# The second stage of a linear-attention and mixture-of-experts block: sixteen groups written out, or six written out and ten in a loop

## The reference

```python
h = layernorm(x) * (1 + ca) + sa                     # x: 2 x 4096 x 512; ca, sa, ga, ... from silu(c) @ wmod
q, k = relu(h @ Wq.T), relu(h @ Wk.T); v = h @ Wv.T  # 16 heads of 32
out = (v' k) q, divided per head by sum(k) . q + 1e-15   # linear attention, no softmax
x1 = x + ga * (out @ w_proj.T + b_proj)
h2 = layernorm(x1) * (1 + cb) + sb
# router: rms norm, logits (8 experts), top 2, softmax weights
# experts: gelu(h2 @ gate) * (h2 @ up) @ down, weighted, summed over the two experts
return x1 + gb * moe(h2)
```

## Time and profile before

| | us |
|---|---|
| median of 3 runs | 2297.94 |
| lowest, highest | 2295.66, 2310.27 |
| the profiled execution | 2295.66 |
| its span, first to last instruction | 2293.9 |
| outside the span | 1.76 |

### The profile page before, as it was taken

How to read it: one execution, slowest core, us unless ns; L and a number is a source line. 1 busy time by engine, 2 the same in 40 slices (tenths; PEclk the granted TensorE clock), 3 DMA queues, 4 the chain that set the end, 5 groups by cost and what they waited for, 6 DMA issues and landing times.

```text
span 2293.9 us, 42231 instructions
## 1 busy us (share of the span) xinstructions
PE 2143.8 (93%) x9280; PEld 1632.9 (71%) x9281; DVE 1437.1 (63%) x3325; ACT 774.7 (34%) x1395; POOL 893.9 (39%) x684
## 2 busy tenths in 40 slices
PE   7999999999988999984899999999989989999997
PEld 5688878888655555552678887887778768778886
DVE  6555555555389999995356565665556556566664
ACT  4243434444334444442132222332223223223332
POOL 4475746656437777775011111111111111111111
PEclk9999999999999999997999999999999999999998
DMA  7576454565625665557755557557675785665554
GB/s 243 205 239 204 163 194 162 210 205 180 216 74 186 218 223 209 186 179 285 219 131 126 125 127 221 131 130 188 156 221 128 190 249 134 180 170 126 131 118 78
DMA packets 292793, 404.88 MB, mean 177 GB/s; under 512 B 50126, under 2 KB 188366, under 8 KB 284878
## 3 DMA queue, kind: packets, MB, share of 16 engines
q1 hardware_dynamic: 164720, 257.57, 35.0%
q0 software_dynamic: 30640, 74.29, 15.3%
q10 hardware_dynamic: 97200, 70.82, 9.6%
HBM read 210.57 MB, written 191.98 MB: 175 GB/s over the span
## 4 chain that ended last, share of the span: by engine, by line
PE 41%; DMA 6%; issue 2%; DVE 1%; ACTq 1%; SPq 1%; ACT 0%; DVEq 0%; POOL 0%
PE bank L1793 41%; DMA arow<-act_rows 3%; DMA act_rows<-hact 3%; ACTq L1044 1%; DVE hact L1682 0%; DMA wbuf<-expert_split 0%; SPq L552 0%; DVE gbr L1718 0%; DVE x_t_lo L1676 0%; DVE act_t_lo L1693 0%; DVEq L1700 0%; ACT gact L1033 0%; DMA expert_rows<-rows,dest 0%; DMA meta<-expert_rows 0%; SPq L550 0%
## 5 line engine op out<-in xcount | busy, mean ns | idle before, releaser
L1793 PE MATMUL bank<-wbuf,x_t_hi 128*128 x2160 | 682.2, 398 | 45.0 <-DVE x_t_lo L1676 41.3
L787 POOL DMA_INDIRECT out_rows<-orow,cur_tok x135 | 209.0, 1548 | 990.0 <-DVE orow L1721 891.0
L1793 PEld LDWEIGHTS bank<-wbuf,x_t_hi 128*128 128x128 f32 x2160 | 410.5, 190 | 139.6 <-issue 49.4
L1793 PE MATMUL bank<-wbuf,x_t_lo 128*128 x1080 | 426.0, 394 | 0.0
L1793 PE MATMUL bank<-wbuf,act_t_hi 128*128 x1080 | 346.7, 403 | 33.3 <-DVE act_t_lo L1693 33.1
L1682 DVE TENSOR_TENSOR hact<-bank,gact 128x512 f32<-128x512 f32 x135 | 93.3, 691 | 335.2 <-PE bank L1793 303.7
L1793 PEld LDWEIGHTS bank<-wbuf,act_t_hi 128*128 128x128 f32 x1080 | 208.1, 193 | 83.4 <-issue 37.8
L1793 PEld LDWEIGHTS bank<-wbuf,x_t_lo 128*128 128x128 f32 x1080 | 205.1, 190 | 47.3
L1793 PE MATMUL bank<-wbuf,act_t_lo 128*128 x540 | 215.9, 400 | 0.0
L1033 ACT ACTIVATE gact<-bank 128x512 f32<-128x512 f32 x135 | 80.7, 598 | 324.1 <-PE bank L1793 264.2
L750 POOL DMA_INDIRECT expert_rows<-rows,dest x128 | 133.8, 1046 | 105.3 <-DVE dest L1458 70.7
(11 more groups left out here) (224 smaller groups left out, 4102.2 us busy)
## 6 DMA issues: line engine op xcount, KB each, us to landing
wbuf<-expert_split SPq DMA_DIRECT2D x24, 1536.0 KB, 8.8
xrow<-expert_rows SPq DMA_DIRECT2D x540, 64.0 KB, 2.8
act_rows<-hact ACTq DMA_DIRECT2D x135, 256.0 KB
arow<-act_rows ACTq DMA_DIRECT2D x540, 64.0 KB
expert_split<-split_hi SPq DMA_DIRECT2D x32, 768.0 KB, 3.5
expert_split<-split_lo SPq DMA_DIRECT2D x32, 768.0 KB, 5.8
xg<-in_x SPq DMA_DIRECT2D x16, 1024.0 KB, 5.6
q_rows<-qf SPq DMA_DIRECT2D x16, 1024.0 KB, 6.5
```

The lines of the kernel that those rows point to most:

```text
L787: pool.indirect_dma_start(out=out, out_offset=bass.IndirectOffsetOnAxis(cur_tok[at][:, 0:1], 0), in_=orow[at % 2][:, :], in_offset=None, c ...
L1793: last = mm(dst, stationary(a, f), moving(b, f), start=(k == 0), stop=(k == parts * n - 1))
```

## The change

`run_groups2` now writes out groups 0 to 2 and 13 to 15, and runs groups 3 to 12 as five turns of a loop with two groups in each. In the loop g is a register, so:

- the values of the waits are worked out by register operations in front of the instructions that wait;
- the batch is `(g >> 3) & 1`, and what is chosen by it (`gab`, `modbc`, `kvp`) is addressed by a register;
- `denominators` no longer reads `ksums` of the batch. VectorE copies the batch's key sums into a new tile `ksum_now` (128 x 64) once for each group (`ksum_of`), and TensorE waits for that copy (`ksum_ready`) in place of the wait on `prep_step`. In a group, `ksum_of(g + 2)` stands between `rec_lo(g + 1)` and `residual(g, 0)`, and waits until the denominators of group g + 1 are done, since there is one tile. For groups 0 and 1 it stands ahead of the first group. There are 16 copies.

No arithmetic on the data changes.

```diff
@@ run_groups2 @@
-        for g in range(NG):
+        for g in range(3):
+            group2(g, g % 2)
+        with eng.Fori(1, (NG - 4) // 2) as j:
+            group2(2 * j + 1, 1)
+            group2(2 * j + 2, 0)
+        for g in range(NG - 3, NG):
             if before_last and g == NG - 1:
                 before_last()
             group2(g, g % 2)
@@
     def batch_of(g):
-        return g // GPB
+        return g // GPB if isinstance(g, int) else (g >> 3) & 1
@@ add_bias (POOL) @@
-                pool.tensor_tensor(xb[par][:, t, :], xb[par][:, t, :], gab[:, batch_of(g), :], ALU.add).then_inc(s_xb, 1)
+                b = batch_of(g)
+                row = gab[:, b, :] if isinstance(b, int) else gab[:, bass.ds(b, 1), :].rearrange("p a n -> p (a n)")
+                pool.tensor_tensor(xb[par][:, t, :], xb[par][:, t, :], row, ALU.add).then_inc(s_xb, 1)
@@ VectorE @@
+        def ksum_of(g):
+
+            at_least(dve, s_den, g)
+            if isinstance(g, int) and g == 2:
+                dve.wait_ge(s_prep, 3)
+            b = batch_of(g)
+            dve.tensor_copy(ksum_now[:, :, :], ksums[:, b, :, :] if isinstance(b, int) else
+                            ksums[:, bass.ds(b, 1), :, :].rearrange("p a f h -> p (a f) h")).then_inc(s_ksum, 1)
@@ mod_row_of (VectorE) @@
-            return modbc[:, batch_of(g), k, :]
+            b = batch_of(g)
+            return modbc[:, b, k, :] if isinstance(b, int) else modbc[:, bass.ds(b, 1), k, :].rearrange("p a n -> p (a n)")
@@ group2 (VectorE) @@
             if not last:
                 rec_lo(g + 1)
+            if has(g, 2):
+                ksum_of(g + 2)
             residual(g, 0, par)
@@ ahead of the groups (VectorE) @@
+        ksum_of(0)
+
         tt(rw[:, :, :], rw[:, :, :], rscale[:, :].unsqueeze(2).to_broadcast([P, FC, E]), ALU.mult).then_inc(s_prep, 1)
         for a in range(HG):
             kvp_of(0, a)
         kvp_lo(0)
+        ksum_of(1)
         recip(0)
@@ denominators (TensorE) @@
-            pe.wait_ge(s_prep, 3 if batch_of(g) else 1)
+            pe.wait_ge(s_ksum, g + 1)
@@
-                last = mm(D_B[0:HEADS, :], ksums[:, batch_of(g), f, :], qb[par][:, f, :], start=(f == 0), stop=(f == FC - 1))
+                last = mm(D_B[0:HEADS, :], ksum_now[:, f, :], qb[par][:, f, :], start=(f == 0), stop=(f == FC - 1))
@@ project (TensorE) @@
-                    lambda k, f: kvp[k][:, b, f, :]).then_inc(s_y, 1)
+                    lambda k, f: kvp[k][:, b, f, :] if isinstance(b, int) else
+                    kvp[k][:, bass.ds(b, 1), f, :].rearrange("p a n -> p (a n)")).then_inc(s_y, 1)
```

More of the change, by code:

```diff
@@ L202, in build @@
     xb.append(sb(ph2, "xb1", [P, TPG, C], F32))
+    ksum_now = sb(ph2, "ksum_now", [P, FC, HEADS], F32)
     sel_f = sb(ph2, "sel_f", [HEADS, C], F32)
@@ L290, in build @@
         sem("kvp_ready"), sem("kvp_hi_ready"), sem("kvp_lo_ready"), sem("sel_ready"))
-    s_q2, s_x2, s_x1st = sem("q_back"), sem("x_back"), sem("x1_stored")
+    s_q2, s_x2, s_x1st, s_ksum = sem("q_back"), sem("x_back"), sem("x1_stored"), sem("ksum_ready")
     s_den, s_dene, s_aden, s_rec0, s_recstep, s_rec, s_rechi, s_reclo, s_rb, s_on = (
@@ L380, in batch_of @@
     def batch_of(g):
-        return g // GPB
+        return g // GPB if isinstance(g, int) else (g >> 3) & 1
+    assert GPB == 8
     def phase1_over(eng):
@@ L735, in number_rows @@
         def number_rows(g, par):
-            if g:
+            if not isinstance(g, int) or g:
                 wait_apart(pool, s_rowm, 2 * g)
@@ L760, in group2 @@
                 low_on(g + 1, 1 - par, 3)
-                if g == 0:
+                if isinstance(g, int) and g == 0:
                     add_bias(g + 1, 1 - par)
-            if g:
+            if not isinstance(g, int) or g:
                 scatter(g - 1, 1 - par)
@@ L970, in group2 @@
         def group2(g, par):
-            before_it = g > 0
+            before_it = not isinstance(g, int) or g > 0
             if before_it:
@@ L1460, in group2 @@
         def group2(g, par):
-            router = g > 0
+            router = not isinstance(g, int) or g > 0
             last = not has(g, 1)
@@ L1477, in group2 @@
             sums(g, 1)
-            if g == 1:
+            if isinstance(g, int) and g == 1:
                 kvp_lo(1)
@@ L1969, in logits_of @@
             if a == 0:
-                pe.wait_ge(s_dene, min(g + 3, NG))
+                pe.wait_ge(s_dene, min(g + 3, NG) if isinstance(g, int) else g + 3)
             for f in range(FC):
```

## The result

| | us |
|---|---|
| changed kernel, median of 4 runs (lowest, highest) | 2332.06 (2321.98, 2332.95) |
| kernel before, median of 4 runs on the same chip | 2302.31 |
| ratio, 95% interval | 1.0117, 1.0072 to 1.0165 |
| predicted, range | 2312, 2299 to 2327 |
| the profiled execution of the changed kernel, its span | 2350.13, 2348.0 |

The change makes the kernel 1.2% slower, 27 us by the ratio and 30 by the medians, and the time lies 5 us above the range. Measured twice more, in two later sets of runs on two chips, it was 1.0112 (1.0084 to 1.0139) and 1.0146 (1.0125 to 1.0167) of the kernel before.

A forecast was written before the change was run, and what follows sets the result against it. VectorE was taken to bound the second stage. Copy 1.8, register operations 4.5 less 1.0 coming back, and back edges 8.8 made 14.1 us, added to the 2297.94 us median for 2312, range 2299 to 2327.

The forecast's parts named there:

- copy: VectorE's `ksum_now` copy, one in each of groups 0 to 13 at 0.13 us: 1.8 us, bounds 1.0 to 2.8.
- register operations, less what comes back: VectorE's loop: 0.45 us in each of ten groups, 4.5 us, less 1 us from shorter waits for TensorE's projection.
- back edges: VectorE's four taken loop branches: instructions fetched again, each next turn 2.2 us late, 8.8 us; bounds 0 to 21.6.
- The bound of 21.6 us (a miss twice): Upper bound for VectorE's back edges: 2.7 us twice in each turn, if the turn's next stretches are missing too.
- `dest` to `rows`: End of a VectorE group: two register operations, each with a wait, make 0.07 us into 0.27, 0.20 more.
- the step behind the logits: On VectorE behind the scaling of the logits: one register operation step showing, 0.07 us more in a group.
- `rec_hi`'s round trip: VectorE's wait for ScalarE's `rec_hi`: two register operations on ScalarE add 0.06 us in every group.
- Rival 1: VectorE's loop stays in its instruction store, so no fetch at back edges: 5.3 us left, 2303; chance 0.36.
- Rival 2: VectorE's register operations are not covered: all 52 in a group cost 44 us, 2344, or 2353 with misses; chance 0.09.
- rival 3: TensorE becomes the bound through register addresses in its projection and its own branch stalls: 2318 to 2330; chance 0.06.
- Rival 4: Faster by a shorter program, with fewer instructions to bring in: 2297 at best; chance 0.02.
- the wait of `rec_lo`: Sign in VectorE's profile: `rec_lo`'s wait grown by as much as the back edge's pause, once in every two groups.

The follow-up runs named there:

- the square: Four kernels on one chip, VectorE's loop or not, the other engines' loop or not: 0.9999, 1.0007, 1.0132 and 1.0146 of the kernel before.
- copy: Changed kernel without any loop, all sixteen groups written out, `ksum_now` copy kept, first chip: 0.9996 of the kernel before.
- copy2: Changed kernel without any loop, `ksum_now` copy kept, measured again on the second chip: 0.9999 of the kernel before.
- mid_in: Changed kernel with VectorE's loop cut in mid-group, behind `mask`, lying over three stretches of 128 instructions: 1.0045 of the kernel before.
- dve_out2: Changed kernel with VectorE's groups written out, loop kept on the other four engines, second chip: 1.0007 of the kernel before.
- mid_out: Changed kernel with VectorE's loop cut behind `mask` and moved by 74 instructions, over four stretches of 128: 1.0097 of the kernel before.
- again2: The changed kernel unaltered, its third measurement, whose profile has none of ScalarE's pauses: 1.0146 of the kernel before.
- pad40: Changed kernel with VectorE's loop moved by 40 instructions of already met waits behind the first stage, first chip: 1.0044 of the kernel before.
- plain: The kernel before itself, unchanged, run again on a third chip that took 2314 us: 1.0013 of the kernel before.
- after: The changed kernel unaltered, its first measurement and profile: median 2332.06 us, 1.0117 of the kernel before.
- dve_only: Changed kernel with the loop on VectorE alone, all other engines written out, first chip: 1.0129 of the kernel before.
- dve_only2: Changed kernel with the loop on VectorE alone, all other engines written out, second chip: 1.0132 of the kernel before.

## Why the prediction was wrong

The forecast's sum was 14.1 us. Of the 20 us between 2312 and 2332.06, 4.4 are the fourth run of the kernel before, which moved its median from 2297.94 to 2302.31; for the rest the sum is too low. On the chip of the square the changed kernel was 0.0146 x 2299 = 33.6 us above before. The terms:

| step | predicted | measured |
|---|---|---|
| copy | 1.8 | not told from 0 (copy, copy2) |
| register operations, less what comes back | 3.5 | 10 (mid_in, 0.0045 x 2297; some 2 of it on the other engines, dve_out2) |
| back edges | 8.8 | 23 (1.0146 less 1.0045; some 6 to either side by the intervals) |

**Back edges, mis-sized.** The mechanism was right: the fourth stretch, only just entered, has the loop fetched again in every turn, and 40 instructions of shift take that away. The step that failed is "the next turn's `rms_var` starts at 724.9 + 2.7 + 0.1 = 727.7": the fetch was mis-sized, at 2.7 us where it took 5.5 to 6.5. I took SyncE's 2.7 us from a place where the DMA share is 0.23 (1245.7 to 1248.4 us) and used it where it is 1.0. For the stretch behind that point the trace of before answers

```profile
724.90:730.90 6.00, 5.99 (x30) 4.52 (x29) 4.97 (x14) 3.24 (x10) 4.73 (x5) 1.00 1.02 366
```

so the row was to be had. In a quiet place it is 2.7 on VectorE too (mid_out). In groups from `x1` to `x1`, those with a pause take 31.5 us in the mean in again2 and 26.8 in pad40, those behind one 27.8 and 26.4: 4.8 and 1.4, times four 25 us, near the 23 of the timed runs. So most of the loss is the pause, and a fifth comes behind it. From a group behind a pause in again2, then the same operations in pad40:

```profile
910.59 1.04 DVE L1340 TENSOR_TENSOR ln<-ln 128x2 f32<-128x2 f32 x1 [0.67 <-ACT ln L948]
911.55 1.85 DVE L1361 SCALAR_TENSOR_TENSOR lnt<-x,mv,modbc 128x512 f32<-128x512 f32 x1
913.33 1.22 DVE L1345 SCALAR_TENSOR_TENSOR ln<-ln,ln 128x2 f32<-128x2 f32 x1
```

```profile
842.12 0.18 DVE L1342 TENSOR_TENSOR ln<-ln 128x2 f32<-128x2 f32 x1
842.22 0.74 DVE L1363 SCALAR_TENSOR_TENSOR lnt<-x,mv,modbc 128x512 f32<-128x512 f32 x1
842.88 0.15 DVE L1347 SCALAR_TENSOR_TENSOR ln<-ln,ln 128x2 f32<-128x2 f32 x1
```

Three operations take 3 us more together, while GpSimd runs `on_lo` (from 910.31, 2.54 us in its timeline) and the additions behind it (from 912.82); in pad40 it only issues scatters there. About half of this is won back later in the group, which is 1.4 us longer in the mean. That GpSimd is the cause is read from the times, not tried. The bound of 21.6 us (a miss twice) comes near by luck: there is one long miss for each turn and not two, and the range left that bound out.

**Register operations, too low.** Of the places that I named, these show in pad40, which has no fetch:

```profile
829.88 0.16 DVE L1337 TENSOR_SCALAR ln<-mv 128x2 f32<-128x2 f32 x1
829.98 0.75 DVE L1363 SCALAR_TENSOR_TENSOR lnt<-x,mv,modbc 128x512 f32<-128x512 f32 x1
...
832.46 0.17 DVE L1480 CAST dest<-destf 128x8 uint32<-128x8 f32 x1
832.67 1.42 DVE L1370 SCALAR_TENSOR_TENSOR rows<-lnt,ln,modbc 128x512 f32<-128x512 f32 x2
...
835.32 0.20 DVE L1375 TENSOR_SCALAR rms<-ss 128x4 f32<-128x4 f32 x1
836.62 0.70 DVE L1285 TENSOR_TENSOR rec_lo<-rec,rec_hi 16x512 fp32r<-16x512 f32 x1 [1.10 <-ACT rec_hi L935]
```

`dest` to `rows` is 0.21 (predicted 0.27, before 0.07), the step behind the logits 0.18 in place of 0.10 (predicted 0.07 more), and one that I had missed is the row of `modbc` for `centred`, 0.10 to 0.23 in place of 0.07. `rec_hi`'s round trip did not grow: the wait is 1.10 in place of 1.03, but `rms_var` ahead of it is 0.20 long and not 0.28, and from start to start it is 1.30 here and 1.31 in the earlier trace rows (predicted 0.06 more). Together these places make about 0.3 us in a group, where the forecast had 0.45. Between the first and the last `rms_var`, though, pad40 and copy2 differ by 8.5 us and mid_in and copy2 by 10.9, so more than half of the loss stands elsewhere. I had looked for none of it. VectorE's waits for the logits, in copy2 and then in pad40:

```profile
DVE route L1386 <- PE bank L2003: 0.6, 2, 0.5
```

```profile
DVE x L1320 <- PE bank L1820: 9.6, 10, 4.1
...
DVE route L1393 <- PE bank L2010: 17.3, 11, 2.1
```

In copy2 the two `rows` operations ahead of the logits overlap with GpSimd and take 1.2 to 1.8 us each from start to start, where 0.65 is the time of one alone; in pad40 they no longer do, and VectorE stands still until TensorE's logits come. The one takes the place of the other, and the sum of the two is 0.15 us longer in a group. The largest single row is an operation of `route` on the mask, which takes 1.13 us from start to start in five groups of pad40 and seven of mid_in, and 0.09 to 0.12 in all of copy2's: 5.2 and 7.3 us. It is no plain price either, since dve_out2, without VectorE's loop, has it nine times and is only 2.9 us longer than copy2. How such overlaps add up to the loss is not shown. The wait for the projection, 9.6 us, gave nothing back (8.2 in the earlier trace rows). By the Trainium skill's queue of eight (Advanced Engine Details and Errata, Engine Queue Depths) I had thought that all of these places might be covered; the 0.21 in place of 0.07 shows that they are not.

**The copy** stands 0.10 us ahead of `x1`, and the time shows nothing of it: 385.1 (copy2) and 386.8 us (copy) from the first to the last `rms_var`, against 386.5. The forecast's 1.8 us would be a ratio of 1.0008, which lies inside both intervals, so it is neither confirmed nor excluded.

**The rivals.** Rival 1 is what the kernel would be 40 instructions further on, though at 1.0045 and not at 2303. Rival 2 (all 52 register operations seen, 44 us) and rival 3 (TensorE the bound) did not come as such: TensorE's wait for `mask` is 32.8 us, though its logits are now waited for. Rival 4 did not come either. Of the signs that I named, the wait of `rec_lo` did not grow; the pause stands ahead of `rms_var`, as "issue". Groups 3 to 12 of pad40, without a fetch, take 26.5 us in the mean, 0.6 above the kernel before as I had said; in again2 those behind a pause take 27.8, some 2 us above that kernel, just at the point at which I had called the forecast wrong.

**Open:** why TensorE's signal for the transposes comes late in some executions (the first that the changed kernel was profiled in, and those on the two chips with 2314 us), and why a kernel whose loop needs no fetch has it most. Wherever the trace has the signal of a paused copy, the copy starts at most 0.03 us behind it, and the signal comes up to 4.7 us behind the recorded end of the transposes; in the ten profiles without pauses it never does. TensorE's signals for the projection come late there too, in `plain` as well, by up to 3 us. Since the ends of matmuls are modelled, the trace does not tell whether the transposes or only their signal is late. The square fell on a chip without these pauses, so it says nothing of them.

## What to carry to other kernels

For a loop on VectorE as here, count over how many stretches of 128 instructions the body lies, and move it (by idle instructions, by where it is cut, or by a shorter body) until it lies over three at most; then look at what the DMA engines do at the back edge, since a fetch cost 2.7 us in a quiet place and some 6 in a full one. Price a stall by the load at the place where it will stand, not at the place where it was seen. Here the version without the loop (1.000) is the best, and a loop on all engines but VectorE (1.001 to 1.002) is nearly free.

## What the runs showed of the hardware that I had not expected

- Three stretches of 128 instructions stay in VectorE's store and four are fetched anew in each turn, though by the count only 5 to 17 instructions of the fourth are used: 15 instruction packets from 800 to 990 us against none on one chip, and 1.0097 (1.0080 to 1.0115) against 1.0045 (1.0028 to 1.0061) on another.
- A taken branch that misses takes 2.7 to 2.8 us at a DMA share of 0.01 (mid_out), 5.5 to 6.5 us at 0.95 to 1.02 (again2, after), and 6.6 to 7.0 us at 1.02 with the loop on VectorE alone (dve_only, dve_only2).
- Waits that are long met start 0.098 us apart on VectorE (41 of them take 4.3 us in pad40), so 62 would take 6.1; the four rows of 62 that met scatters took 6.3 to 10.3 us.
- The kernel before takes 2297 to 2299 us on two chips and 2314 on two others. On the latter TensorE's signals come up to 4.6 us behind the recorded ends of its transposes, and ScalarE's copies start 0.02 us behind the signal.
